# An fp32 perceiver block: GpSimd subtracts the low parts of the attention's tail units, and gate and up multiply high weights by 480 columns of high and low tokens

## The reference

```python
x = x + xattn(layernorm(x))      # keys and values: 1601 context rows of each sequence, then its own 64 tokens
x = x + attn(layernorm(x))       # 16 heads of 64, rotary positions, causal
x = x + ffn(layernorm(x))        # 8 experts

# xattn, for each sequence b (one head, 1024 wide)
scores = q @ concat([ctx[b], x @ wk.T]).T / 32
out    = softmax(scores) @ concat([ctx[b], x @ wv.T]) @ wo.T

# ffn
weights = golden_weights(x, Wr, temperature)      # (token, expert), zero for most pairs
gate = einsum('btd,edf->betf', x, Wg)
up   = einsum('btd,edf->betf', x, Wu)
h    = silu(gate) * up
out  = einsum('bte,betd->btd', weights, einsum('betf,efd->betd', h, Wd))
```

## Time and profile before

| | us |
|---|---|
| median of 3 runs | 1269.14 (1261.7, 1269.14, 1269.29) |
| the profiled execution | 1264.38 |
| its span, first to last instruction | 1262.6 |
| the attention over the context | about 108 to 440 |
| output projection, self-attention, router | about 440 to 709 |
| experts, some 68 each | 709 to 1262 |

### The profile page before, as it was taken

How to read it: one execution, slowest core, us unless ns; L and a number is a source line. 1 busy time by engine, 2 the same in 40 slices (tenths; PEclk the granted TensorE clock), 3 DMA queues, 4 the chain that set the end, 5 groups by cost and what they waited for, 6 DMA issues and landing times.

```text
span 1262.6 us, 19328 instructions
## 1 busy us (share of the span) xinstructions
PE 1200.4 (95%) x7810; PEld 1050.4 (83%) x7810; DVE 818.9 (65%) x1026; ACT 633.1 (50%) x604; POOL 95.7 (8%) x74
## 2 busy tenths in 40 slices
PE   5999999999998999999997699999999999999996
PEld 5888777777777878888886698989898999999895
DVE  7336789989999566463565674747565655656465
ACT  4124889888897423123543345344444444454431
POOL 0010000000000000000000012121111111121202
PEclk9999899999999999999999799999999999999998
DMA  7445899999998624220234376766667666676642
GB/s 290 146 159 192 308 352 360 376 373 363 379 383 333 248 77 171 96 100 34 101 143 167 113 251 166 262 197 226 202 216 212 200 227 200 217 210 230 172 160 33
DMA packets 46872, 272.98 MB, mean 216 GB/s; under 512 B 5880, under 2 KB 6024, under 8 KB 18528
## 3 DMA queue, kind: packets, MB, share of 16 engines
q1 hardware_dynamic: 36768, 243.48, 52.8%
q0 software_dynamic: 10048, 28.71, 9.4%
HBM read 255.92 MB, written 16.25 MB: 216 GB/s over the span
## 4 chain that ended last, share of the span: by engine, by line
PE 77%; DVE 8%; ACT 6%; issue 4%; DMA 4%; POOLq 0%; SPq 0%; POOL 0%; ACTq 0%; DVEq 0%
PE ps L1426 21%; PE ps L1427 21%; PE ps L1428 21%; PE ps L1539 6%; DVE lo L939 5%; ACT hi L628 4%; DMA out<-y,target 3%; PE ps L1652 2%; PE ps L1903 1%; PE ps L1587 1%; DVE stats L943 1%; ACT scores L692 1%; DMA raw<-weights 1%; PE ps L1745 1%; PE ps L1729 1%
## 5 line engine op out<-in xcount | busy, mean ns | idle before, releaser
L939 DVE TENSOR_TENSOR lo<-raw,hi 128x2048 fp32r<-128x2048 f32 (+1 forms) x198 | 443.4, 2251 | 160.3 <-ACT hi L628 157.9
L628 ACT ACTIVATE hi<-raw 128x2048 fp32r<-128x2048 f32 (+1 forms) x198 | 370.5, 1882 | 252.2 <-PE ps L1428 241.3
L1426 PE MATMUL ps<-act_hi,hi 128*128 128x240 f32 (+2 forms) x1232 | 360.7, 293 | 7.4 <-DVE act_lo L965 4.1
L1428 PE MATMUL ps<-act_hi,lo 128*128 128x240 f32 (+2 forms) x1232 | 361.6, 294 | 0.0
L1427 PE MATMUL ps<-act_hi,hi 128*128 128x240 f32 x1024 | 282.8, 276 | 0.0
L1426 PEld LDWEIGHTS ps<-act_hi,hi 128*128 128x128 f32 x1232 | 234.2, 190 | 16.7 <-issue 5.4
L1428 PEld LDWEIGHTS ps<-act_hi,lo 128*128 128x128 f32 x1232 | 234.6, 190 | 6.9
L1427 PEld LDWEIGHTS ps<-act_hi,hi 128*128 128x128 f32 x1024 | 193.5, 189 | 0.3
L1426 PE MATMUL ps<-hi,act_hi 128*128 128x512 f32 x320 | 126.4, 395 | 0.0
L1428 PE MATMUL ps<-hi,act_lo 128*128 128x512 f32 x320 | 124.9, 390 | 0.0
L1427 PE MATMUL ps<-lo,act_hi 128*128 128x512 f32 x320 | 124.8, 390 | 0.0
(11 more groups left out here) (228 smaller groups left out, 1431.2 us busy)
## 6 DMA issues: line engine op xcount, KB each, us to landing
raw<-weights SPq DMA_DIRECT2D x124, 1024.0 KB, 4.9
raw<-keys SPq DMA_DIRECT2D x36, 1024.0 KB, 5.8
raw<-context SPq DMA_DIRECT2D x31, 1024.0 KB, 8.3
raw_more<-context SPq DMA_DIRECT2D x17, 1024.0 KB
raw_more<-keys SPq DMA_DIRECT2D x12, 1024.0 KB
xq<-x_in SPq DMA_DIRECT2D x4, 512.0 KB, 6.8
raw_more<-weights SPq DMA_DIRECT2D x4, 512.0 KB
new_keys_t<-kvs POOLq DMA_DIRECT2D x8, 256.0 KB, 3.6
```

What stands on the lines that cost most here:

```text
L628: act.activation(part(hi, k, kind), part(raw, k, kind), ACT.Copy).then_inc(hi_done, 1)
L939: dve.tensor_tensor(part(lo, k, kind), part(raw, k, kind), part(hi, k, kind), ALU.subtract).then_inc(lo_done, 1)
L1426: pe.matmul(out, a_hi, b_hi, start=first, stop=False)
L1428: return pe.matmul(out, a_lo, b_hi, start=False, stop=last)
```

## The change

1. In the attention the low parts of the 16 tail units go from VectorE's queue to GpSimd's, with a semaphore of their own, `tail_lo`. TensorE, and SyncE for the buffer's next load, wait for it.
2. `exps(0)` moves on ScalarE's queue behind the split that followed it.
3. Gate and up: for each of the 16 weight tiles of a unit one matmul of 480 columns (high weights, the tokens' high and low parts side by side) and one of 240 (low weights, high parts). Gate and up have a PSUM bank each, f even in banks 0 and 1, f odd in 6 and 7. The product with the tokens' low parts lies in columns 240 to 479: ScalarE copies these of both to SBUF (`gu_copied`), VectorE adds columns 0 to 239 (`gu_added`), ScalarE takes Silu from SBUF, and VectorE goes on as before. The SBUF tile lies in the part of `xq` that held x.
4. What the banks bring with them: the down projection's first half uses banks 0 and 1, and waits for `h_split` of blocks 6 and 7 instead of 3 and 7; at the end of an expert TensorE waits for its `y`; ScalarE waits for the first store of the output; TensorE waits for the first list to be read (`first_listed`).

```diff
@@ sync: load @@
-                    sp.wait_ge(lo_done, last + 1 + per * i)
+                    if kind_of(last) in (KEY_LAST, VALUE_LAST):
+                        sp.wait_ge(tail_lo, tails_before(last + 1))
+                    else:
+                        sp.wait_ge(lo_done, last + 1 - tails_before(last) + per * i)
@@ gpsimd, between the stores of the new keys and the load of x @@
+            for n in range(len(ATTENTION)):
+                k = U_KEYS0 + n
+                kind = kind_of(k)
+                if kind not in (KEY_LAST, VALUE_LAST):
+                    continue
+                pool.wait_ge(hi_done, k + 1)
+                if kind == KEY_LAST:
+                    (lo_a, lo_b), (raw_a, raw_b), (hi_a, hi_b) = (tail_parts(a, k) for a in (lo, raw, hi))
+                    pool.tensor_tensor(lo_a, raw_a, hi_a, ALU.subtract)
+                    pool.tensor_tensor(lo_b, raw_b, hi_b, ALU.subtract).then_inc(tail_lo, 1)
+                else:
+                    pool.tensor_tensor(part(lo, k, kind), part(raw, k, kind), part(hi, k, kind),
+                                       ALU.subtract).then_inc(tail_lo, 1)
...
-        Y_BANK = (6, 2)
+        Y_BANK = (0, 2)
+        GU_BANK = (0, 6)
@@ scalar: attention @@
                     if what == "keys":
                         s = b - 1
+                        if u == 0 and s == 0:
+                            exps(0)
...
                                 copied += 1
-                                exps(0)
@@ scalar: item @@
                     if k < 8:
+                        bank = GU_BANK[k % 2]
                         act.wait_ge(gu_ready, 8 * e + (k + 1))
-                        act.activation(silu[:, k % 2, :], ps[:, k % 2, 0:CAP], ACT.Silu).then_inc(silu_done, 1)
+                        if k >= 2:
+                            act.wait_ge(h_split, 8 * e + (k - 1))
+                        act.activation(gate_up[:, k % 2, :, :], ps[:, bank:bank + 2, CAP:2 * CAP],
+                                       ACT.Copy).then_inc(gu_copied, 1)
+                        act.wait_ge(gu_added, 8 * e + (k + 1))
+                        act.activation(gate_up[:, k % 2, 0, :], gate_up[:, k % 2, 0, :], ACT.Silu).then_inc(silu_done, 1)
...
             turned_hi(0)
+            act.wait_ge(scattered, 16)
@@ vector: split @@
+                if kind in (KEY_LAST, VALUE_LAST):
+                    return
                 dve.wait_ge(hi_done, k + 1 + per * i)
@@ vector: item @@
                     if k < 8:
+                        bank, both = GU_BANK[k % 2], gate_up[:, k % 2, :, :]
+                        gate, up = both[:, 0, :], both[:, 1, :]
+                        dve.wait_ge(gu_copied, 8 * e + (k + 1))
+                        dve.tensor_tensor(both, ps[:, bank:bank + 2, 0:CAP], both, ALU.add).then_inc(gu_added, 1)
                         dve.wait_ge(silu_done, 8 * e + (k + 1))
-                        steps.done(dve.tensor_tensor(silu[:, k % 2, :], ps[:, k % 2, CAP:2 * CAP],
-                                                     silu[:, k % 2, :], ALU.mult))
+                        steps.done(dve.tensor_tensor(gate, up, gate, ALU.mult))
@@ tensor: item @@
                     elif f == 0:
                         pe.wait_ge(routed, 1)
+                        pe.wait_ge(first_listed, 1)
...
-                            ins = three(ps[:, f % 2, j * CAP:(j + 1) * CAP], hi[:, k % RING, at], lo[:, k % RING, at],
-                                        xg[:, c, 0:CAP], xg[:, c, CAP:2 * CAP], c == 0, c == C - 1)
+                            out = ps[:, GU_BANK[f % 2] + j, 0:2 * CAP]
+                            if c == C - 1:
+                                pe.matmul(out[:, 0:CAP], lo[:, k % RING, at], xg[:, c, 0:CAP], start=False, stop=False)
+                            ins = pe.matmul(out, hi[:, k % RING, at], xg[:, c, 0:2 * CAP], start=c == 0, stop=c == C - 1)
+                            if c < C - 1:
+                                pe.matmul(out[:, 0:CAP], lo[:, k % RING, at], xg[:, c, 0:CAP], start=False, stop=False)
...
-                            pe.wait_ge(h_split, 8 * e + 4 * (half + 1))
+                            pe.wait_ge(h_split, 8 * e + (7 + half))
...
+                if more:
+                    pe.wait_ge(y_done, 4 * e + 3)
```

More of the change, by code:

```diff
@@ L241, in perceiver_block @@
         lo_done = sem("lo_done")
+        tail_lo = sem("tail_lo")
         unit_used = sem("unit_used")
@@ L310, in perceiver_block @@
         xg_done = sem("xg_done")
+        first_listed = sem("first_listed")
+        gu_copied = sem("gu_copied")
+        gu_added = sem("gu_added")
         gu_ready = sem("gu_ready")
@@ L385, in perceiver_block @@
                                           for j in range(3))
-        silu = xq[:, TT * D:TT * D + 2 * CAP].rearrange("p (s n) -> p s n", s=2)
+        gate_up = xq[:, 0:4 * CAP].rearrange("p (s j n) -> p s j n", s=2, j=2)
         spare = xq[:, TT * D:TT * D + 2 * TT * NE * NE].rearrange("p (s n) -> p s n", s=2)
@@ L414, in landing, with part, half_tile, blocks_before @@
             return landed[slots[u]], 16 * (counts[u] + PER_EXPERT // RING)
+        def part(buf, k, kind):
+            whole = raw_of(k) if buf is raw else buf[:, k % RING, :]
+            if kind == KEY_LAST:
+                return whole[:, 0:C * (KTAIL + QL)]
+            if kind == VALUE_LAST:
+                return whole[0:KREM, 0:D]
+            if kind == BLOCK:
+                return whole[:, 0:D]
+            return whole
+        def half_tile(buf, h):
+            return buf[:, 4 * (h % 2):4 * (h % 2) + 4, (h // 2) * P:(h // 2 + 1) * P]
+        def blocks_before(n):
+            return sum(what == "block" for what, _, _ in ATTENTION[:n])
+        def tail_parts(buf, k):
+            whole = part(buf, k, KEY_LAST)
+            if buf is raw:
+                return (whole[:, 0:C * KTAIL].rearrange("p (c n) -> p c n", c=C),
+                        whole[:, C * KTAIL:].rearrange("p (c n) -> p c n", c=C))
+            by_chunk = whole.rearrange("p (c n) -> p c n", c=C)
+            return by_chunk[:, :, 0:KTAIL], by_chunk[:, :, KTAIL:]
+        def tails_before(k):
+            return sum(kind_of(m) in (KEY_LAST, VALUE_LAST) for m in range(U_KEYS0, min(k, U_WO)))
+        def kind_of(k):
+            if not U_KEYS0 <= k < U_WO:
+                return FULL
+            what, b, u = ATTENTION[k - U_KEYS0]
+            if what == "block":
+                return BLOCK
+            return FULL if u < 6 else (KEY_LAST if what == "keys" else VALUE_LAST)
         block = ctx.enter_context(nc.Block())
@@ L1294, in _ @@
             dve.wait_ge(list_summed, 1)
-            dep(dve.tensor_copy(listed[0:R, :, 2:LIST], ps[0:R, FIRST_BANK, 0:NT * 8].rearrange("p (n k) -> p n k", k=8)
-                                [:, :, 2:LIST]))
+            dve.tensor_copy(listed[0:R, :, 2:LIST], ps[0:R, FIRST_BANK, 0:NT * 8].rearrange("p (n k) -> p n k", k=8)
+                            [:, :, 2:LIST]).then_inc(first_listed, 1)
+            dve.wait_ge(first_listed, 1)
             def slot_values():
@@ L1422, in unit_ready @@
             def unit_ready(k, per=0, i=0):
-                pe.wait_ge(lo_done, k + 1 + per * i)
+                if kind_of(k) in (KEY_LAST, VALUE_LAST):
+                    pe.wait_ge(tail_lo, tails_before(k + 1))
+                else:
+                    pe.wait_ge(lo_done, k + 1 - tails_before(k) + per * i)
             def three(out, a_hi, a_lo, b_hi, b_lo, first, last):
```

37 lines of the change are left out of this document (3 added, 34 removed).

## The result

| | kernel before | changed kernel |
|---|---|---|
| runs, us | 1261.7, 1264.5, 1269.14, 1269.29 | 1277.99, 1280.31, 1281.66, 1286.63 |
| median, us | 1266.82 | 1280.99 |
| ratio | 1 | 1.0138, 95% interval 1.0111 to 1.0166 |
| profiled execution, us (span) | 1264.4 (1262.6) | 1280.3 (1278.5) |

The changed kernel is slower by 1.4%, where the forecast was "no change that can be told", 1271 us. The profiled executions differ by 15.9 us where the sum said +4. I first laid marks that both kernels have against each other. The last exp of the attention starts at 393.94 before and at 399.93 after, 6.0 us late. TensorE's first matmul of the experts starts at 709.46 and 715.11, 5.65 late, and from there to the end it is 553.1 and 563.4 us, 10.3 more. So both the attention (forecast -2 with the first exp) and the experts (forecast +6) came out dearer.

A forecast was written before the change was run, and what follows sets the result against it. TensorE was taken to bound the experts, with unit 2 starting when VectorE's chain ends; in attention, the chain of waits through ScalarE and TensorE. Terms +6 + 3 - 1 - 4 = +4 gave 1268.4 to 1273.1, stated 1271 us, range 1252 to 1288.

The forecast's parts named there:

- Part 1, 480 columns: Gate and up matmuls: a unit costs 5.20 us instead of 5.39, gaining 0.19, or 12 us on 64 units.
- The lower bound, "none": Gate and up units: no gain if 480 columns are as dear as 512.
- Part 2, the chain at the turn: Expert turns: VectorE's longer chain delays unit 2 by 1.08 us and the list by 0.9; expert part +6 us in all.
- Part 3, tails: Attention tails on GpSimd: VectorE waits for GpSimd in five middle steps, 0.6 x 5 = +3 us; key tails -1 us.
- The last key tail's -1: Last key tail of the attention: two pieces of 0.6 us leave VectorE's chain, -1 us.
- Part 4, the first exp: First exp behind the next split: TensorE goes on 1.85 us sooner, waits 0.9, the clock stays up: -4.0 us.
- The sum: Whole kernel: +6 + 3 - 1 - 4 = +4 us on the profiled execution's 1264.4; forecast 1271 us, chance 0.60 within 1%.
- Rival "VectorE paces the attention": Attention: all 2.4 us a step come back over seven steps, -17 us, giving 1252; chance 0.18.
- Rival "GpSimd is much slower": Value tails of steps 1 to 5: at 4.5 us a subtract +14 us, giving 1285; decides from 3.8 us; chance 0.12.
- Rival "the clock falls in the longer wait": Waits before unit 2 at seven turns: clock falls, seven times 3 us, giving 1292; chance 0.10 for most turns.

The follow-up runs named there:

- e8_turn_reordered: Changed kernel with tails back on VectorE, edits of e5_wait_for_add and e6_late_target, and unit 0's copy and add ahead of unit 3's split: 1250.71 us, ratio to before 0.9882.
- e9_before_with_turn: Kernel before with first exp moved, target rows behind hidden block 2, unit 0's Silu and hidden block ahead of unit 3's split, 240-column matmuls kept: 1254.78 us, ratio 0.9948.
- e1_tails_only: Kernel before with only the tails' low parts moved to GpSimd: 1269.48 us, ratio to before 1.0052.
- e11_all_parts_turn: Changed kernel, tails on GpSimd, with the edits of e8_turn_reordered at the turn: 1258.51 us, ratio to before 0.9961.
- e5_wait_for_add: e3_gate_up_only with TensorE waiting, from unit 2, for VectorE's add instead of the hidden block's low part, and taking the next list behind unit 3: 1254.38 us, ratio 0.9914.
- e6_late_target: e3_gate_up_only with VectorE computing an expert's target rows behind hidden block 2 instead of ahead of everything: 1269.41 us, ratio to before 1.0035.
- e2_exps_only: Kernel before with only the first exp moved behind the next split: 1262.78 us, ratio to before 0.9988.
- e3_gate_up_only: Changed kernel with tails and first exp put back as before, so only gate and up are changed: 1276.74 us, ratio to before 1.0101.
- e10_tails_behind_vector: e1_tails_only with GpSimd taking a value tail only when VectorE is done with the unit ahead of it: 1270.43 us, ratio to before 1.0059.
- e7_value_tails_in_quarters: e1_tails_only with each value tail's GpSimd subtract cut into four of 65x256: 1278.17 us, ratio to before 1.0100.

## Why the forecast was right or wrong, step by step

- **Part 1, 480 columns: the mechanism right, the size wrong.** A pair steps at 0.333 us, not 0.325 (six pairs from 853.98 to 855.98), so by the periods of e8_turn_reordered and e9_before_with_turn a unit gains 0.076 us, not 0.19, and 64 units 4.9 us, not 12. Step that failed: "480 columns cost 212.6 ns". In units 3 to 7 of expert 3 the 480-column matmul steps at 222.5 ns in the mean, 4 below the 512-column row, and the 240-column one behind it at 110.7, about as forecast. It was not the line through zero that was at fault: one through both rows, 240 at 112.3 and 512 at 226.8, gives 213.3 for 480. The step lay in taking any line between streams of one width for the price in a mixed pair; why 480 columns are so near to 512's there stays open. The lower bound, "none", was nearer than my value.
- **Part 2, the chain at the turn: right.** Unit 2 starts 4.94 us behind the target (forecast 4.9), 1.14 us later than before (1.08). TensorE waits for the selections in experts 0 to 6, the list coming 0.7 to 0.8 us late (0.9), but in expert 2 not, whose wait before unit 2 had used it up. The Silu table load ran ahead of its wait. Units 3 to 7 run at TensorE's pace, at 5.32 us where 5.20 were foreseen, which is Part 1's miss again. A plain turn costs +1.57 us (69.48 against 67.91) instead of +0.85, and nearly all of the difference is the six units of Part 1, 6 x 0.11.
- **Part 3, tails: right in steps 1, 3 and 5, wrong in 2 and 4.** GpSimd takes 2.42 us alone (taken 2.3), and where it comes behind VectorE the next split is 0.5 us late (0.6). Step that failed: "In the middle steps GpSimd gets the port at 206.63, when VectorE's split ends", read from one step and taken times five. The timeline of before shows that the steps alternate: in step 2 the tail's high part ends at 242.31 and VectorE's split starts at 242.63; in step 3 it ends at 279.96 and the split starts at 279.93. Where GpSimd is first, VectorE stands 2.2 us, TensorE 3.3, and the clock falls: 4.1 and 5.3 us in the changed kernel. From the second exp to the last the tails cost 8.9 us there, 6.4 in e1_tails_only and 7.5 in e11_all_parts_turn (against e8_turn_reordered), where +2 was forecast; the rest of the difference was not taken apart. By the Trainium skill, "SBUF — State Buffer", section "Who interferes with whom", who issues first holds the pair for the whole instruction and the order decides who blocks; the trace agrees, with 4.42 us on GpSimd in one order and 4.48 on VectorE in the other. The last key tail's -1 did not come as I put it: its first piece took 3.33 us (2.0 of them a wait for VectorE), and a `tensor_scalar` of VectorE's beside the second took 1.14 us instead of 0.25. With key tails only, the last score unit came 1.7 us sooner than before, but 1.3 of these stand already at the second exp, as in e5_wait_for_add and e6_late_target (1.2 and 1.5), which move no tail. Behind it, 0.4 us is left for all key tails.
- **Part 4, the first exp: the mechanism right, the size taken from one execution.** By the second exp it is -2.9 us in the changed kernel and -3.2 in e2_exps_only (forecast -4), with a wait of 0.75 for the split in the changed kernel (0.9). The clock over 138 to 144 is 1.00 there as forecast, but 0.92 in e2_exps_only and 0.84 in e8_turn_reordered, so the fall isn't always avoided. And the 3.1 us that I put on the fall were those of one execution, in which it lasted longest; against six kernels with a shorter fall there, e2_exps_only gains 1.6 to 2.3 us. I took TensorE to turn its weights until 135.4, which it does after a wait of 1.33 for the exp. Of the gain, -1.5 (-4.3 to +1.3) reaches the end.
- **The sum.** Attention +2 - 4 was forecast at -2 and came out at +6.0 by the last exp; experts +6 came out at +10.3. The whole was forecast at +4 and came out at +15.9. That 1281 us lies within 1252 to 1288 speaks for no step of the sum: its upper end was priced with a slow GpSimd, which did not come true. That rival's 1285 us and the 1281 measured lie near each other by chance.
- **Rival "VectorE paces the attention": out.** Its 20 us of relief are gone from VectorE and nothing is faster; e1_tails_only is +6.6.
- **Rival "GpSimd is much slower": not by its speed** (2.42 against the 3.8 from which it was to decide), but +3 was too little all the same (the tails cost +6.6 in e1_tails_only, and 8.9 in the changed kernel's trace), since in two steps the whole instruction is in the way and not its excess over a gap.
- **Rival "the clock falls in the longer wait": right in one turn of the changed kernel and three of e3_gate_up_only.** What I missed is what makes the wait long: not the chain's constant 1.1 us, but a late scatter on top of it. That could also explain why the runs lie between 1278.0 and 1286.6, against 1253.5 and 1256.3 in e5_wait_for_add; it is shown for the profiled executions only.

## What to carry to other kernels

When work is moved to GpSimd beside a VectorE that is nearly full, don't compare its length with the gap in one step: look in every step of the pattern for which of the two is ready first, and price both orders, since the engine that comes second stands until the other's instruction is over. That the right order alone makes it free was not found here (e10_tails_behind_vector). Before a matmul is made cheaper at the price of a longer chain behind it, look for what TensorE really needs from that chain: here it waited for a hidden block when only its banks had to be free, behind a target that only a later store needs, and with both waits on the right event the change to gate and up gave 11 us instead of costing 13, some 5 of them by the matmuls. A price for a width that no row has isn't safe on a line between two widths: here it was 213 ns on the line and 222 in the trace, and most of the hoped gain went with that. The safe bound was the next wider row.

## What the runs showed of the hardware

- Cutting a GpSimd instruction into four made it slower as a whole: 65x1024 took 2.41 us in one, and four of 65x256 took 2.85 us with the port free and 6.9 to 7.1 beside VectorE's splits, for VectorE took the port between two of them.
- At the turns TensorE's granted clock fell from 2.4 to 1.2 GHz behind waits of 2.02, 2.74, 2.75 and 4.06 us in the changed kernel and e3_gate_up_only, behind 1.94 in e10_tails_behind_vector and behind 1.75 in e7_value_tails_in_quarters. It stayed behind 1.78 (changed kernel), 1.92 (e2_exps_only), 2.03 (e1_tails_only) and 2.38 us (e7_value_tails_in_quarters), and behind every shorter wait at a turn. Full turns with a fall took 1.8 to 3.5 us longer than a plain one, the longer wait included. In the attention it fell behind the waits of 3.3 us, but in the changed kernel also at 288, where no single wait was above 1.1 us. The wait's length alone doesn't decide it, and what does stays open. Two turns of e7_value_tails_in_quarters, in which the shorter wait had the fall (0.50 from 1214 to 1216) and the longer had none:

```profile
1006.72 0.38 PE L1449 MATMUL ps<-act_hi,hi 128*128 128x240 f32 x1 [2.38 <-DVE h_lo L1415]
...
1212.36 0.35 PE L1449 MATMUL ps<-act_hi,hi 128*128 128x240 f32 x1 [1.75 <-DVE h_lo L1415]
```

- A matmul of 480 columns followed by one of 240 took 0.333 us in a stream without waits, but 0.326 in the unit that followed a wait of 1.48 (937.74 to 942.31, 14 pairs). The periods of e5_wait_for_add, 66.67 to 66.89 us, are likewise up to 0.2 us shorter than those of e8_turn_reordered, which waits for nothing. What makes this difference stays open; no run was made for it.
